# The ends of the last stage: third group loaded inside attention, second matmuls ahead of the last turn, and the last group's sums finished tile by tile

## The reference, cut to what matters

```python
# x: (4, 32, 32, 192), i.e. 4096 tokens of 192 channels
x = x + conv(_ln_c(x))      # "conv" is 12-head attention over 1024 tokens per image,
                            # with decomposed row and column position bias, then out @ Wp + bp
t = x.reshape(4, 1024, 192)
t = t + ffn(_ln_t(t))

def ffn(x0):                # 4-bit fake-quantised, 192 -> 768 -> 192
    xq = round(clip(x0 / mean(alpha_a1), -8, 7))
    x1 = xq @ round(clip(w1 / alpha_w1, -8, 7)).T * alpha_w1 * mean(alpha_a1) + b1
    x1 = clip(gelu(x1), -10, 10)
    hq = round(clip(x1 / mean(alpha_a2), -8, 7))
    return hq @ round(clip(w2 / alpha_w2, -8, 7)).T * alpha_w2 * mean(alpha_a2) + b2
```

## Time and profile before

| | us |
|---|---|
| median of 3 runs | 863.06 (858.8 to 864.1) |
| the profiled execution, its time | 859.48 |
| its span, first to last instruction | 857.7 |
| barrier between attention and last stage | 757.9 to 758.0 |
| last stage | 758 to 857.7 |

### The profile page before, as it was taken

How to read it: one execution, slowest core, us unless ns; L and a number is a source line. 1 busy time by engine, 2 the same in 40 slices (tenths; PEclk the granted TensorE clock), 3 DMA queues, 4 the chain that set the end, 5 groups by cost and what they waited for, 6 DMA issues and landing times. The chain is left out here.

```text
span 857.7 us, 14811 instructions
## 1 busy us (share of the span) xinstructions
PE 767.9 (90%) x5688; PEld 401.1 (47%) x5688; DVE 687.9 (80%) x929; ACT 572.6 (67%) x969; POOL 453.6 (53%) x292
## 2 busy tenths in 40 slices
PE   4969565388999999999999999999999999989975
PEld 2635365244444444444444444444444444347753
DVE  6999765398888888888888888888888888249994
ACT  1233345306877887787777887787788778868773
POOL 2577699317474664837373846557473334512330
PEclk9979878659999999999999999999999999999988
DMA  7756679999959393957769492939487120033411
GB/s 196 214 165 217 207 182 372 377 210 186 190 112 209 70 216 65 217 100 163 153 125 191 88 212 66 207 66 220 92 176 140 55 82 13 13 123 128 151 37 55
DMA packets 65750, 130.02 MB, mean 152 GB/s; under 512 B 9535, under 2 KB 45392, under 8 KB 57224
## 3 DMA queue, kind: packets, MB, share of 16 engines
q1 hardware_dynamic: 57648, 115.95, 58.5%
q10 hardware_dynamic: 8032, 13.13, 4.3%
HBM read 89.73 MB, written 34.60 MB: 145 GB/s over the span
## 5 line engine op out<-in xcount | busy, mean ns | idle before, releaser
L1134 DVE TENSOR_REDUCE at_neg_max<-at_r_ps 128x1 f16<-128x1024 f32 x384 | 451.5, 1217 | 84.7 <-PE at_r_ps L993 84.7
L1088 ACT ACTIVATE at_probs<-at_s_ps 128x512 f32<-128x512 f32 x768 | 410.7, 600 | 92.8 <-PE at_s_ps L1013 92.0
L1013 PE MATMUL at_s_ps<-op_mix_q,op_mix_k 128*128 128x512 f16 x768 | 264.6, 382 | 4.6 <-ACT at_probs L1088 1.6
L993 PE MATMUL at_r_ps<-op_mix_k,op_mix_q 128*128 128x256 f16 (+1 forms) x1920 | 239.1, 257 | 16.7 <-DMA op_mix_q<-bias_parts 12.0
L1025 PE MATMUL at_o_ps<-at_probs,op_v_u 128*32 128x512 f32 x1536 | 204.1, 604 | 0.0
L993 PEld LDWEIGHTS at_r_ps<-op_mix_k,op_mix_q 128*128 128x128 f16 x1920 | 156.8, 100 | 94.1 <-DVE at_neg_max L1134 15.8
L910 POOL COPY op_mix_q<-op_mix_q 2x4096 f16<-2x4096 f16 x48 | 171.6, 3601 | 1.5
L1013 PEld LDWEIGHTS at_s_ps<-op_mix_q,op_mix_k 128*128 128x128 f16 x768 | 74.1, 97 | 166.3 <-issue 69.6
L220 POOL MEMSET op_mix_q<- 2x10240 f32 x12 | 103.5, 8627 | 21.2 <-PE at_o_ps L1025 21.1
L914 POOL TENSOR_TENSOR at_o_sb<-at_o_sb,at_inv_rows 128x512 f32<-128x512 f32 x23 | 29.4, 1280 | 126.5 <-DVE at_inv_rows L1150 125.3
L907 POOL COPY op_mix_q<-op_mix_q 2x1024 f16<-2x1024 f16 x24 | 24.9, 1036 | 107.3 <-ACT op_mix_q L1093 107.3
(11 more groups left out here) (131 smaller groups left out, 682.0 us busy)
## 6 DMA issues: line engine op xcount, KB each, us to landing
op_mix_q<-qk_parts SPq DMA_DIRECT2D x48, 640.0 KB, 11.0
op_mix_q<-bias_parts SPq DMA_DIRECT2D x120, 120.0 KB, 9.6
op_mix_q<-bias_parts SPq DMA_DIRECT2D x72, 128.0 KB, 9.5
qk_parts<-op_mix_q SPq DMA_DIRECT2D x24, 256.0 KB, 2.4
v_rows<-pr_v_st SPq DMA_DIRECT2D x8, 768.0 KB, 4.1
op_mix_k<-qk_parts SPq DMA_DIRECT2D x48, 128.0 KB, 13.3
op_v_u<-v_rows SPq DMA_DIRECT2D x12, 512.0 KB, 14.1
op_mix_q<-bias_parts SPq DMA_DIRECT2D x24, 256.0 KB, 9.7
```

Source lines behind the costliest of these rows:

```text
L993: last = pe.matmul(r_ps[count % RRING][:, first // GROUP, first % GROUP:first % GROUP + n], mix_q[owner.buf][:, variant, j, qt * P:(qt + 1 ...
L1013: pe.matmul(s_ps[use % SRING][:, :], mix_k[unit.buf][:, j, keys], mix_q[unit.buf][:, ops.VARIANT_OF[kt], j, queries], start=True, stop=Tru ...
L1088: act.activation(probs[n % PRING][:, j, :], s_ps[use % SRING][:, :], ACT.Exp).then_inc(s_taken, 1)
L1134: dve.tensor_reduce(neg_max[half][:, j // 2, t, j % 2:j % 2 + 1], r_ps[count % RRING][:, :, :].rearrange("p h t -> p (h t)"), AX_X, ALU.ma ...
```

## The change

Four edits, all in the last stage or in front of it:

1. **Third group inside attention.** After the last unit SP waits for `y_done` = 1 and issues the load of group 2 at the end of the attention block; the last stage's loop no longer does so for its first group.
2. **Order on PE in group 6.** second(5) is issued ahead of turn(7) in place of behind it.
3. **The last group's sums.** second(7) becomes `second_last`: it writes four tiles of sums into four separate banks (`p_ps` at 0 and 2, `h_ps[0]`, `h_ps[1]`) which hold nothing live by then. So it does not wait for stage_c(6) to free `f_ps`. It runs in two parts: bias and the first three hidden blocks of every tile once the first half of `hid_q` is there, then the other three of every tile, with a signal after each tile.
4. **The last group's end.** stage_c(7) becomes `finish_last`: DVE scales tile by tile (128x192), and after each two tiles adds y (128x384) and signals; SP stores each pair (192 KB) by a DMA of its own.

```diff
             each_unit(sp, emit)
+            sp.wait_ge(ffn_in.y_done, 1)
+            ffn_in.load(sp, FIRST.after(2))
...
+        last_f_done, last_scaled, last_res = (ph.sem(n) for n in ("last_f_done", "last_scaled", "last_res"))
+        last_f = [p_ps[:, 0, 0:C], p_ps[:, 2, 0:C], h_ps[0][:, 0:C], h_ps[1][:, 0:C]]
...
-                if not (g.last or g.after(1).last):
+                if not (g.first or g.last or g.after(1).last):
                     sp.wait_ge(y_done, g.n + 1)
                     ffn_in.load(sp, g.after(2))
...
             store(LAST.after(-1))
-            store(LAST)
+            for pair in range(2):
+                tiles = slice(2 * pair, 2 * pair + 2)
+                sp.wait_ge(last_res, pair + 1)
+                sp.dma_start(out_v[LAST.n, :, tiles, :], res[LAST.s][:, tiles, :]).then_inc(stored[LAST.s], 16)
             for s in range(2):
-                sp.wait_ge(stored[s], 16 * (GROUPS // 2))
+                sp.wait_ge(stored[s], 16 * (GROUPS // 2 + (1 if s == LAST.s else 0)))
...
+            def finish_last():
+                s = LAST.s
+                dve.wait_ge(stored[s], LAST.it * 16)
+                for t in range(TILES):
+                    dve.wait_ge(last_f_done, t + 1)
+                    dve.tensor_tensor(ffn[s][:, t, :], last_f[t], wt.s2_row[:, :], ALU.mult).then_inc(last_scaled, 1)
+                    if t % 2:
+                        tiles = slice(t - 1, t + 1)
+                        dve.wait_ge(last_scaled, t + 1)
+                        dve.tensor_tensor(res[s][:, tiles, :], ffn[s][:, tiles, :], y[LAST.n % YRING][:, tiles, :], ALU.add).then_inc(last_res, 1)
+
             each_group(dve, emit)
-            stage_c(LAST)
+            finish_last()
...
+                if g.after(1).last:
+                    second(g.after(-1))
                 if not g.last:
                     turn(g.after(1))
-                if not g.first:
+                if not (g.first or g.after(1).last):
                     second(g.after(-1))
 
+            def second_last():
+                pe.wait_ge(y_done, GROUPS)
+                pe.wait_ge(gelu_done, GROUPS * HT)
+                for part in range(2):
+                    pe.wait_ge(hq_done, LAST.n * 2 + part + 1)
+                    for t in range(TILES):
+                        if part == 0:
+                            pe.matmul(last_f[t], wt.ones[:, :], wt.b2_parts[:, :], start=True, stop=False)
+                        for k in range(part * half_h, (part + 1) * half_h):
+                            last = pe.matmul(last_f[t], hid_q[LAST.s][:, k, t * P:(t + 1) * P], wt.w2_t[:, k, :], start=False, stop=(k == HT - 1))
+                        if part == 1:
+                            last.then_inc(last_f_done, 1)
+
             each_group(pe, emit)
-            second(LAST)
+            second_last()
```

## The result

| | before | after |
|---|---|---|
| median | 863.06 us (857.76 to 864.95, 7 runs) | 855.22 us (852.96 to 855.69, 7 runs) |
| ratio to before | | 0.9908, 95% interval 0.9885 to 0.9931 |
| span of the profiled execution | 857.7 | 853.4 |
| first DVE instruction of the last stage (memset of `magic`) | 758.18 | 761.02 |
| last stage, from there to the end of the span | 99.5 | 92.4 |

The kernel is 0.9% faster. The two profiled spans differ by only 4.3 us, because everything ahead of the last stage took 2.8 us longer in the profiled execution of after. So I compare from the first DVE instruction of the stage on: 7.1 us (99.50 − 92.38, with the spans at two decimals, 857.68 and 853.40).

The account below looks back on a forecast made before the run. DVE bounds the middle of the last stage, chains of waits its last two groups. 0.3 + 3.1 + 2.9 + 0.6 = 6.9 us off the median gives 856.2, off the mean 854.5; forecast between, 855.5, range 851.5 to 859.5.

Parts of the forecast that it names:

- edit 1: Start of the last stage: project(2) waits for no load, so residual(2) starts earlier; gain 0.3 us.
- edit 2: Group 7's turn: second(5) fills PE's hole, so the first GELU comes earlier; gain 3.1 us, ends 2.8 and 3.9.
- edits 3 and 4, to the last sum: Last group: second(7) leaves the chain, last add at B + 7.4, not B + 10.3; gain 2.9 us, ends 2.5 and 3.3.
- the store: End of the kernel: last store of 192 KB lands in 2.0 us, not 2.6; gain 0.6, ends 0 and 0.9.
- the part that the clock takes back: hidden(7): clock falls near the end of the 3.2 us hole before it, taking 0.8 us off a 3.9 us gain.
- the lower end of 2.8: Smallest gain in us expected from second(5) ahead of turn(7), with the clock low from the turn on.
- The case that I had worked out: Last group's sums at 1.2 GHz: fourth tile readable at B + 6.4, its product due at B + 6.44.
- The lower end, a gain of nothing: Last store: fixed DMA cost of about 2 us with 192 KB on top, an estimate of 2.5, almost no gain.
- The rival that ends slower: Attention's end: the early 1152 KB load slows it or SP holds up the barrier; slower or unmoved kernel 0.04.
- edit 1's ends, 0 and 0.3: Start of the last stage: smallest and largest gain in us expected from loading group 2 inside attention.
- The four upper ends: Largest gains for the early load, PE order, last group and store: 0.3, 3.9, 3.3, 0.9 us; sum given as 7.7.

Follow-up runs that it names:

- second trace: The kernel before, unchanged, traced again for its clock at the start of the last stage; last stage 101.31 us.
- third trace: The kernel before, unchanged, traced once more; last stage 100.33 us.
- the run with fillers: The kernel after plus matmuls with unread results in PE's holes (around turn(7), ahead of the last sums); last stage 91.72 us, ratio to before 0.9912.
- the version with halves and all fillers: Kernel after, group 7's GELUs and rounding in halves, stage_c(6) between stage_b(7)'s halves, unread matmuls in PE's holes behind second(5); 852.37 us, 0.9899 of before.

## Why the prediction was right, and where it wasn't

The forecast was 855.5 us and 855.22 was measured. The terms came out so, as the trace of before less that of after, first for the trace that the forecast was worked from, then for the other two:

| step | forecast, us | measured, us | second trace | third trace |
|---|---|---|---|---|
| edit 1 | 0.3 | 0.35 (74.05 − 73.70) | 2.0 | 2.15 |
| edit 2 | 3.1 | 3.2 (12.07 − 8.85) | 3.3 | 1.7 |
| edits 3 and 4, to the last sum | 2.9 | 2.9 (10.28 − 7.37) | 2.9 | 3.5 |
| the store | 0.6 | 0.6 (3.10 − 2.46) | 0.6 | 0.6 |
| sum | 6.9 | 7.1 | 8.9 | 8.0 |

- **Edit 2** is right in its mechanism and in the part that the clock takes back: 0.8 forecast, 0.68 measured against the run with fillers. That the clock falls was the right choice for the trace of after, though not near the hole's end, as I had put it, but 0.3 us after hidden(7) had begun. And it is not the rule: one trace shows no fall, and another one that costs 1.30 us, beyond the lower end of 2.8 (12.07 − 9.47 = 2.6). What edit 2 gives depends on the clock of the old order as well: against the third trace of before it is 1.7.
- **Edits 3 and 4.** The product of 128x192 was put at 0.36 by a straight line between two rows; it took 0.35, and a sum of 128x384 0.56. The chain on DVE, 2.33, took 2.34 (848.60 to 850.94). PE kept ahead of it. The case that I had worked out, all 28 matmuls at 1.2 GHz and the fourth tile ready only just in time, did not come: the first part ran at 2.4 GHz and only the second at 1.2, and its last matmul ended at B + 5.3, not 6.2. The error of the Trainium skill's two formulas is small (VectorE: DVE Perf Modes, section on the TRN2 errata): 0.33 by its table, 0.36 by the other. Its advice against small tiles holds for DVE's own time, 0.4 more; but the split is repaid by what it lets run side by side, 1.9 net where the clock was low.
- **The store** of 192 KB landed 2.0 us behind its issue (two of them, 2.0 and 2.1), as the row of 256 KB had it. The lower end, a gain of nothing, did not come. The Trainium skill's fixed cost of about 2 us (DMA: Bandwidth & Descriptors, Latency and other measured facts) agrees with 2.0 if the transfer is taken as part of it, not as added.
- **The rival that ends slower** is refuted by the stretch that it names: 13.65 us from residual(0) to the stage in every trace.
- **The step that failed is edit 1's ends, 0 and 0.3.** They rest on the 0.24 us that DVE was short of work in one trace. I priced the removed wait only by itself, at the clock that this trace had, although I used a fall of the clock behind an idle PE for edit 2. In four of five traces without edit 1 the clock fell behind this very wait, and edit 1 is worth 2.0 to 2.15 there. So the stage differs by 8.9 and 8.0 us in the other two traces, not by 7.1.
- **A sum in the range is wrong.** The four upper ends, 0.3, 3.9, 3.3 and 0.9, add up to 8.4 and not to 7.7; 7.7 has edit 2 alone at its upper end. The gain was said to lie between 5.3 and 7.7 in nine of ten cases; the medians differ by 7.8, and two of the three traces give more than 7.7.
- **So the total fits partly by luck.** 6.9 us off the median of 863.06 would be 856.2. I went down to 855.5 because the mean of four executions lay lower; but the median of seven is again 863.06. By the traces, what makes up for it is the larger gain of edit 1; in time this is not shown. The difference of the medians is 7.8 us, which the stages of before (99.5, 101.3 and 100.3, mean 100.4) less the one trace of after (92.4), 8.0, account for. How often the fall comes in executions without a trace is not known; five traces are few.

## What to carry to other kernels

A wait on TensorE is to be priced twice: by what its consumer waits for, and by the matmuls behind it at the lower clock, on a stage where a late result is never made up. One trace doesn't show whether a short wait lets the clock fall, so a second and third trace of the kernel before are worth more than a finer reading of the first. At the end of a kernel, where engines wait for one another in turn, split the last piece so that the next engine can begin on its first part, even if each piece then costs more: here 0.4 us more on DVE bought 1.9 with the clock low, and would have bought about 0.5 net with it high, by the estimate above.

## What the runs showed of the hardware

- The granted clock can fall when PE has waited only 1.72 us, and while it is at work again. In the kernel with edit 2 alone it fell at about 765.2 on its time axis (a mean of 0.60 between 765 and 766), 0.3 us after project(2) had begun; with the same wait of 1.72 us at the same place the first trace of before stayed at 2.4 GHz. The Trainium skill speaks of the clock falling after a longer idle time (TensorE: Matmul & The Clock Gate, Part 1); the measured wait is shorter, and hidden(0) in front of it is paced by ACT, so that PE wasn't full there either (its 12 matmuls took 3.41 us, while six fillers of the same size, in the version with halves and all fillers, took 1.46).
- Such a fall is costly for its length: the 24 fp32 matmuls of one projection took 5.85 us in place of 4.07 to 4.17 in each of the four traces that have it.
- Executions differ in their time ahead of the last stage: its first DVE instruction came between 755.2 and 764.6 us, and between 755.2 and 761.1 us in the five traces without edit 1, whose kernels are the same up to there. The cause stays open.
